# Entry of batches 4 to 7 moved into the attention's main loop on VectorE; rows to transpose written ahead of residual rows

## The reference

```
x = x + 0.5 * moe8(layernorm(x));   x = x + attn0(layernorm(x))      # queries 512, keys 256 (convolution, stride 2)
x = x + 0.5 * moe8(layernorm(x));   x = x + 0.5 * block1f(layernorm(x))
x = x + attn1(layernorm(x));        x = x + 0.5 * block1f(layernorm(x))
# block1f: causal attention over layer-normed rows, residual, 16 experts top 2, residual
# moe: softmax gate, top 2 of 8 or 16 experts with a capacity, every row = sum of two weighted expert rows
```

## Time and profile before

| | us |
|---|---|
| median of three runs (2227.15 to 2235.24) | 2228.93 |
| the profiled execution, its own time | 2219.2 |
| its span, first to last instruction | 2217.5 |
| busy: PE, DVE | 1635.7, 1380.3 |
| busy: POOL, ACT | 1014.6, 979.6 |

### The profile page before, as it was taken

How to read it: one execution, slowest core, us unless ns; L and a number is a source line. 1 busy time by engine, 2 the same in 40 slices (tenths; PEclk the granted TensorE clock), 3 DMA queues, 4 the chain that set the end, 5 groups by cost and what they waited for, 6 DMA issues and landing times. The chain is left out here.

```text
span 2217.5 us, 45287 instructions
## 1 busy us (share of the span) xinstructions
PE 1635.7 (74%) x16814; PEld 929.4 (42%) x16816; DVE 1380.3 (62%) x3344; ACT 979.6 (44%) x2064; POOL 1014.6 (46%) x1706
## 2 busy tenths in 40 slices
PE   4434778873637999982687359999999999836872
PEld 3321333332514656651333135555656556523331
DVE  8538667746188777757321497777777777474213
ACT  1112566651214766661222127667666767511220
POOL 1233365530523657430577334536556674305772
PEclk9975899985858999996898669999999999867996
DMA  6242222210432323300244322332323233002444
GB/s 199 65 126 74 57 70 72 76 38 27 139 86 60 103 79 84 103 22 24 62 102 87 104 84 75 92 85 75 103 71 92 79 89 98 22 24 58 95 86 129
DMA packets 226872, 178.20 MB, mean 80 GB/s; under 512 B 33447, under 2 KB 215599, under 8 KB 226272
## 3 DMA queue, kind: packets, MB, share of 16 engines
q1 hardware_dynamic: 211232, 154.74, 24.6%
q0 software_dynamic: 10240, 17.96, 4.0%
q10 hardware_dynamic: 5184, 2.63, 0.4%
HBM read 104.34 MB, written 72.35 MB: 80 GB/s over the span
## 5 line engine op out<-in xcount | busy, mean ns | idle before, releaser
L657 DVE TENSOR_REDUCE mx<-PS 128x2 f32<-128x512 f32 (+3 forms) x1408 | 787.6, 611 | 255.5 <-PE PS L358 171.3
L530 ACT ACTIVATE pt<-PS 128x512 f32<-128x512 f32 (+2 forms) x1408 | 667.1, 533 | 363.7 <-PE PS L358 263.4
L373 PE MATMUL PS<-ka,qa 48*128 48x256 bf16 (+3 forms) x2048 | 503.6, 308 | 86.7 <-DVE mx L657 80.1
L482 PE MATMUL PS<-qa,ka 51*128 51x512 bf16 (+3 forms) x1792 | 485.2, 319 | 31.3 <-DMA qa<-nm 31.2
L358 PE MATMUL PS<-mask_q,identh 64*128 64x128 bf16 (+1 forms) x3072 | 354.9, 206 | 0.0
L427 PE MATMUL PS<-pt,vs 128*32 128x512 f32 (+3 forms) x3584 | 348.6, 482 | 0.0
L358 PE MATMUL PS<-mask_k,identh 64*128 64x64 bf16 (+1 forms) x3072 | 343.3, 202 | 0.0
L1174 POOL DMA_INDIRECT pt<-xn_rows,idx x160 | 165.3, 1033 | 333.7 <-DVE idx L1109 286.1
L767 POOL CAST nm<-nm 16x128 bf16<-16x128 f32 x128 | 36.0, 281 | 593.3 <-ACT nm L562 581.2
L358 PEld LDWEIGHTS PS<-mask_k,identh 64*128 64x128 bf16 x3072 | 270.3, 95 | 54.1 <-issue 1.8
L358 PEld LDWEIGHTS PS<-mask_q,identh 64*128 64x128 bf16 x3072 | 275.3, 97 | 26.5 <-issue 6.8
(11 more groups left out here) (212 smaller groups left out, 2363.0 us busy)
## 6 DMA issues: line engine op xcount, KB each, us to landing
pt<-in_f_w SPq DMA_DIRECT2D x96, 256.0 KB, 3.2
q_parts<-parts SPq DMA_DIRECT2D x192, 128.0 KB, 2.4
qa<-q_parts SPq DMA_DIRECT2D x256, 96.0 KB, 2.4
k_parts<-parts SPq DMA_DIRECT2D x144, 128.0 KB, 2.4
ka<-k_parts SPq DMA_DIRECT2D x192, 96.0 KB, 2.4
xn_rows<-xn SPq DMA_DIRECT2D x32, 256.0 KB, 2.3
xn<-y_rows SPq DMA_DIRECT2D x32, 256.0 KB, 4.8
hid<-y_rows SPq DMA_DIRECT2D x32, 256.0 KB, 5.4
```

The costliest lines, as they stand in the source:

```text
L373: mm = pe.matmul(PS[:, bank, i * n:(i + 1) * n], k.qa[rows, b % 2, g, h // 2, qb * P:(qb + 1) * P], k.ka[rows, b % 2, g, h // 2, 0:n], sta ...
L482: mm = pe.matmul(PS[:, bank, i * n:(i + 1) * n], k.ka[rows, b % 2, g, h // 2, kb * P:(kb + 1) * P], k.qa[rows, b % 2, g, h // 2, q0:S], st ...
L530: nc.scalar.activation(k.pt[:, u % 2, at[c]:at[c] + len(heads) * n], PS[:, SC_BANK + c % RING, 0:len(heads) * n], ACT.Exp, scale=SCORE_SCA ...
L657: nc.vector.tensor_reduce(out, PS[:, MX_BANK + t % RING, 0:len(heads) * n] .rearrange("p (h n) -> p h n", n=n), AX.X, ALU.max).then_inc(s. ...
```

## The change

Batches 4 to 7 are no longer entered between the max tiles of units 0 and 1. Batch 4 is entered in unit 1 of the main loop, 5 in unit 2, 6 in unit 5 and 7 in unit 6, each in three steps: the first set of products at slot 8, the second at slot 10, the moments at slot 11 (attention 1: slots 5, 6 and 7). The inverse roots of all four are computed at slot 0 of unit 7. `norm` writes the rows that TensorE transposes (`xa`) ahead of the residual rows (`hid`), under a signal of their own. GpSimd adds the biases of batches 0 and 1 before it splits the queries of batch 1.

```diff
+    LATE_ENTRY = {1: 4, 2: 5, 5: 6, 6: 7}
...
+        if u in LATE_ENTRY:
+            events += [(name, LATE_ENTRY[u]) for name in ("late0", "late1", "late2")]
+        if u == max(LATE_ENTRY) + 1:
+            events += [("late_root", 3)]
...
+            def entry(step, b):
+                if step < 2:
+                    combine(nc, k, dve, seg(b).src, b, step)
+                else:
+                    dve.wait_ge(*s.combined.at(2 * b + 2))
+                    chain.link(moments(nc, k, chain, seg(b).src, b))
...
-                if twice:
-                    normalise(nc.vector, k, src, b, k.rstd, lambda t: here(dst, b)[:, t * P:(t + 1) * P])
                 normalise(nc.vector, k, src, b, k.rstd2 if twice else k.rstd,
                           lambda t: k.xa[:, t, :]).then_inc(s.xa_ready.h, 1)
+                if twice:
+                    normalise(nc.vector, k, src, b, k.rstd,
+                              lambda t: here(dst, b)[:, t * P:(t + 1) * P]).then_inc(s.base_ready.h, 1)
...
             enter(2)
-            for t in range(NMX):
-                max_tile(0, t)
-            enter(3)
-            for t in range(NMX):
-                max_tile(1, t)
+            for u in range(2):
+                for t in range(NMX):
+                    max_tile(u, t)
...
             for g in range(G):
                 spread(0, g)
+            add_bias(0)
+            add_bias(1)
             split(0, 1)
...
-                if u == 0:
-                    add_bias(0)
-                    add_bias(1)
```

More of the change, by code:

```diff
@@ L286, in attention @@
         when = {"value_p": 2, "max_T": 2, "o_out": 2, "nm": 2, "o_T": 5, "value0": 8, "x_T": 8, "k": 8, "ctx_T": 8,
-                "q": 11, "v": 11, "out": 11, "value1": 11, "moments": 4, "f_moments": 4, "f_T": 8, "f_l": 11}
+                "q": 11, "v": 11, "out": 11, "value1": 11, "moments": 4, "f_moments": 4, "f_T": 8, "f_l": 11,
+                "late0": 8, "late1": 10, "late2": 11, "late_root": 0}
         early, late = ((0,), (1,)), (2, 3)
@@ L292, in attention @@
         when = {"value_p": 2, "max_T": 2, "o_out": 2, "nm": 2, "o_T": 4, "x_T": 5, "k": 5, "ctx_T": 5, "value0": 6,
-                "q": 7, "v": 7, "out": 7, "moments": 3, "f_moments": 3, "f_T": 5, "f_l": 7}
+                "q": 7, "v": 7, "out": 7, "moments": 3, "f_moments": 3, "f_T": 5, "f_l": 7,
+                "late0": 5, "late1": 6, "late2": 7, "late_root": 0}
         early, late = ((0,),), (1,)
@@ L596, in _, with entry_deviations @@
             chain = Chain(dve, s.ln_step)
+            def entry(step, b):
[4 more added lines that the diff above has]
+                    chain.link(moments(nc, k, chain, seg(b).src, b))
+            def entry_deviations(group):
+                first, n = ENTRY_GROUPS[group]
+                deviations(nc, k, chain, columns(first, n), seg(0).twice).then_inc(s.st_ready.h, 1)
             def enter(group):
@@ L601, in enter @@
                 for b in range(first, first + n):
[L602 to L606, removed]
+                    for step in range(3):
+                        entry(step, b)
+                entry_deviations(group)
             def later_moments(b):
@@ L717, in _ @@
                         tail(name, n)
+                    elif name in ("late0", "late1", "late2"):
+                        entry(int(name[-1]), n)
+                    elif name == "late_root":
+                        entry_deviations(n)
                     elif name == "moments":
@@ L796, in add_bias @@
             def add_bias(b):
-                pool.wait_ge(*s.xa_ready.at(b + 1))
+                pool.wait_ge(*(s.base_ready if seg(b).twice and b < 2 else s.xa_ready).at(b + 1))
                 base = here(seg(b).dst if seg(b).twice else seg(b).src, b).rearrange("p (t c) -> p t c", c=C)
@@ L899, in attention @@
     counts = {
[L900 removed]
+        s.ln_step: k.entry_steps, s.pl_step: k.pool_steps, s.st_ready: len(ENTRY_GROUPS), s.mo_ready: NB - B, s.fm_ready: B - 1,
+        s.base_ready: 2 * seg(0).twice, s.combined: 2 * B, s.xn_stored: 16 * B,
         s.xa_ready: NB, s.ob_added: NB, s.xT_full: NB, s.xT_free: NB, s.q_full: NB,
@@ L1240, in __init__ @@
         self.ln_step = new("ln_step")
-        self.pl_step = new("pl_step")
+        self.pl_step, self.base_ready = new("pl_step"), new("base_ready")
         self.st_ready, self.mo_ready, self.fm_ready = new("st_ready"), new("mo_ready"), new("fm_ready")
```

## The result

| | us |
|---|---|
| kernel before, median of 20 runs beside the changed one | 2233.51 |
| changed kernel, median of 20 runs | 2222.74 |
| ratio, 95% interval | 0.9939, 0.9914 to 0.9964 |
| changed kernel, the profiled execution, its own time | 2225.7 |
| its span | 2224.0 |

The ratio puts the change at 13.6 us faster, between 8 and 19; it is taken over fast runs alone, without one run of the kernel before that took 5129 us, and the medians differ by 10.8 us. The forecast was 23.2 us, and a time of 2205.7; the measured time lies outside the range of 2191 to 2220. Of the miss of 17.0 us in the time, 4.6 us are the kernel before itself, which took 2233.51 us here and 2228.93 when the forecast was made. The direction was right and the size was not.

What follows compares the result with a forecast made beforehand. VectorE was taken to bound the prologue and TensorE the main loops, most fully in attention 2. 47.5 - 21.9 - 3.9 + 1.5 = 23.2 us faster gave 2205.7 us, range 2191 to 2220.

Steps and rivals of the forecast that it cites:

- head start: Start of the three main loops: max tile 0 of unit 2 starts 13.0, 18.4 and 16.1 us earlier, 47.5 us.
- bias additions: Prologue: GpSimd's additions slow VectorE's products of batches 2 and 3 by 1.3 us per attention block, 3.9 us lost.
- clock at the loops' start: Main loops' start: without the idle time TensorE may be at the upper clock there, 1.5 us gained.
- given back in the loops: Main loops: moved products and roots exceed VectorE's idle time where they are put and delay TensorE, 21.9 us lost.
- upper end: Bias additions in the prologue: VectorE stands still for both, 2.5 us per attention block, up to 7.5 us.
- first pair: Units 1 and 2 of attention 2: 7.34 us moved against 4.91 idle, 2.4 us late.
- the balance: Main loops: VectorE's lateness is moved work less its idle time from the insertion to the first tiles after, 21.9 us.
- the last rival: Loop: moved products meet GpSimd, up to 1.74 us more for each of 24 sets; 19 us slower, 2248 us; chance 0.07.
- gaps at the wrong place: Loop: bursts block the ring before idle time is reached, a third of moved work hides; 9.6 us faster, 2219 us; chance 0.20.
- slower through GpSimd: Loop: product sets meeting GpSimd cost up to 1.74 us more each; 19 us slower, 2248 us; chance 0.07.
- A new wait in the start: Blocks' start: SP's queue takes back 6 us more per block; 5 us faster, 2224 us; chance 0.05.

Runs made afterwards that it cites:

- roots at slot 8: Changed kernel with the roots of attentions 2 and 3 after the ninth maximum of unit 7 instead of at slot 0; ratio to the kernel before 0.9903.
- rows first alone: Kernel before with only `xa` written ahead of the residual rows in attention 2, the bias additions waiting for the residual rows; ratio 0.9998.
- TensorE kept busy: Changed kernel with 36 repeats of a score product ahead of score chunk 4 of unit 7, attentions 2 and 3; ratio to the kernel before 0.9977.

## Why the prediction was off

| term of the sum, us | forecast | measured | read from |
|---|---|---|---|
| head start | 47.5 | 47.1 | tile 0 of unit 2, 41.0 earlier, plus the additions |
| bias additions | -3.9 | -6.1 | first maximum; taken back, 6.0 |
| clock at the loops' start | +1.5 | -1.9 | unit 0, 39.1, less 41.0 |
| given back in the loops | -21.9 | -25.5 | unit 0 to unit 10 |
| sum | 23.2 | 13.6 | |

**Head start.** Right, and so was its reason: the keys' loads, not VectorE, set it; putting them first brought that tile 5.5 us and unit 0 7 us forward.

**Bias additions.** The step that failed: "the additions are fewer instructions than the split, so I take 1.3 us". The number of instructions is no measure; their length is: the set beside them in attention 2 took 2.0 us more, and they last 2.65. The better price stood in the same paragraph as an upper end.

**The clock.** The step that failed: "without the idle time it may be at the upper level there". The sign was wrong. The clock came back at 675.3 us in attention 2, 10.9 us earlier than before, but the loop began 14.6 us earlier, so more of it ran at half speed. In attention 3 it is the same (6.7 us at half speed now, 3.3 before). The -1.9 is a remainder; by half of 3.4 us in each of two blocks it would be -3.4.

**What the loops give back.** Attention 1 gave back 3.7 (4.4 forecast), attention 3 8.0 (8.0), attention 2 13.8 (9.3). In attention 2 the first pair cost about 1.4 us (2.4 forecast) and the second, with the roots, 12.5 (6.9). In attention 3 the pairs cost 2.2 and 5.7 (3.3 and 4.7): products alone cost less than the balance says, and roots more, so that its 8.0 is right by luck: two errors that cancel. The term that failed is "the 19 root steps of attention 2 cost 3.86 us": measured 7.1, for the steps met GpSimd's splits, then a wait of 6.8 us and about 10 us at half clock. In attention 3, where the steps were hardly longer, the same burst brought a wait of 1.5 us and 7 us at half clock. The prediction had no term for the clock in the loop. It did weigh GpSimd in the loop, but for products alone, and by GpSimd's mean busy time in a stretch; it did not look at what GpSimd does at slot 0. The moved products themselves took 1.13 or 1.14 us a set in attentions 2 and 3, and in attention 1 two sets took 1.95, so the last rival did not happen.

**The rivals.** None of them describes what came. The time of "gaps at the wrong place" (2219 us) is nearest, and "slower through GpSimd" named the mechanism at the wrong instructions. "A new wait in the start" is small: the wait for keys is 1.53 us in attention 2.

**What stays open.** In the profiled executions the ends of the blocks differ by several us, and the clock with them: in the changed kernel TensorE is at half speed from about 982 us to the end of attention 2, which costs 8.3 us that neither the kernel before nor the kernel with the roots at slot 8 shows. Six of the ten profiles of kernels with the change have it and neither of the two without it, which is too few to tell whether it belongs to the change. In attention 1 the lead of 8.5 us at unit 10 is gone by the last unit, but rows first alone, with attention 1 as before, is 9.3 us behind there, so the one profile of the kernel before was a quick one in that place. The runs without a profile say that this is common: in the 20 runs of the changed kernel time goes with the mean granted clock. The eleven above 2222 us have 0.848 to 0.859, the nine below 2216 us 0.862 to 0.874. The two profiled executions are 0.866 for the kernel before and 0.854 for the changed one, so the changed one was taken at the lower clock, and looks longer. What sets the clock in one execution isn't known. That the clock's fall in unit 7 costs up to 5 us is worked out from the granted clock; at the 2.0 us for 7 us that the two profiles of the changed kernel show, an estimate is 3 us, and no run separated it from the wait.

## What to carry to other kernels

Before moving a chain of short dependent steps to another slot, look at what the neighbour engine does in that slot, instruction by instruction: its length there can be twice that of where it stood, and a gap seen in the profile may close once the kernel runs on time. When idle time is to hold moved work, two pieces side by side may cost what one costs, up to a point that a run has to find. A block that starts earlier may start at the lower clock, so a head start is worth less than its length.

## What was not expected of the hardware

A step of 128x16 elements took up to 1.0 to 1.2 us instead of 0.17 beside GpSimd instructions, with two tensors as input and with one: `TENSOR_SCALAR` was held as well (743.46, and 753.04 in the kernel with the roots at slot 8). The granted clock fell to 0.50 at about 739 us in the kernel with TensorE kept busy, and the records, in which the ends of matmuls are modelled, show TensorE busy throughout the stretch in which it fell and the two behind (3.00 of 3.00 us each; 2.34 of 3.00 in the one ahead). So a full busy share in the profile is no assurance of the full clock.
